# A perceiver layer on one core: written-out engine orders behind the cross-attention, a third score bank, and low parts of two shared blocks on GpSimd

## What is computed

```python
def _L0_xattn_ref(image_features, text_features, Wq, bq, Wk, bk, Wv, bv):
    ...
    scores = jnp.einsum('bqh,bkh->bqk', query, key) * scale
    weights = jax.nn.softmax(scores, axis=-1)
    attended = jnp.einsum('bqk,bkh->bqh', weights, value)
...
def _L0_attn_ref(x, W_dq, W_uq, q_ln_g, q_ln_b, W_dkv, W_ukv, kv_ln_g, kv_ln_b, W_o):
    ...
    cq = _layernorm(x @ W_dq, q_ln_g, q_ln_b)
    Q = cq @ W_uq
    ckv = _layernorm(x @ W_dkv, kv_ln_g, kv_ln_b)
    KV = ckv @ W_ukv
    ...
    scores = scores * mask
    scores = jnp.where(scores == 0, -jnp.inf, scores)
    attn = jax.nn.softmax(scores, axis=-1)
    out = jnp.einsum('bhqk,bkhd->bqhd', attn, v).reshape(B, S, D)
    return out @ W_o.T
...
    x = x + _L0_xattn_ref(_layernorm(x, axis=-1), ctx_768, ...)
    x = x + _L0_attn_ref(_layernorm(x, axis=-1), ...)
    x = x + _L0_ffn_ref(_layernorm(x, axis=-1), ...)
```

## Time and profile before

| | us |
|---|---|
| median of three runs | 369.08 |
| lowest, highest | 368.37, 370.68 |
| the profiled execution | 367.66 |
| its span | 365.9 |
| TensorE busy | 338.9 |

### The profile page before, as it was taken

One profiled execution on the slowest core, in us unless ns is written; L12 is line 12 of the kernel. 1 busy time (PEld: TensorE's weight loads), 2 busy tenths in 40 slices (PEclk: granted clock), 3 DMA queues, 4 the chain that ended last, 5 costly groups with the idle time before them and its releaser, 6 DMA issues.

```text
span 365.9 us, 6976 instructions
## 1 busy us (share of the span) xinstructions
PE 338.9 (93%) x2530; PEld 237.4 (65%) x2530; DVE 244.2 (67%) x481; ACT 190.9 (52%) x429; POOL 83.2 (23%) x103
## 2 busy tenths in 40 slices
PE   5999989999999989987959789999999999999996
PEld 3998666677777767766748667988644444444344
DVE  1874879646588467647675665993436677778587
ACT  2466675526557476355555561522036677777520
POOL 3600000000010211402332304004337544432000
PEclk9999999999999999998978899999999999999999
DMA  7984499976322246055000056479935553331573
GB/s 233 375 322 166 153 391 419 387 231 233 111 88 87 89 134 269 29 219 241 3 28 0 31 172 261 198 275 420 377 141 180 169 174 126 117 107 59 199 291 115
DMA packets 17185, 69.70 MB, mean 190 GB/s; under 512 B 2816, under 2 KB 3328, under 8 KB 14592
## 3 DMA queue, kind: packets, MB, share of 16 engines
q1 hardware_dynamic: 12768, 56.93, 41.7%
q0 software_dynamic: 3520, 11.54, 8.9%
q10 hardware_dynamic: 864, 0.79, 0.7%
HBM read 61.91 MB, written 7.34 MB: 189 GB/s over the span
## 4 chain that ended last, share of the span: by engine, by line
PE 76%; DVE 11%; ACT 6%; issue 3%; DMA 2%; POOL 1%; ACTq 0%; DVEq 0%
PE bank L1802 10%; PE bank L1388 10%; PE bank L1770 10%; PE bank L1390 9%; PE bank L1389 9%; PE bank L1643 8%; PE bank L1739 2%; ACT hw L831 2%; PE bank L1531 2%; PE bank L1781 2%; PE bank L1813 2%; DVE cT L1147 2%; DMA bq_s<-in_bq 2%; PE bank L1613 2%; PE bank L1541 1%
## 5 line engine op out<-in xcount | busy, mean ns | idle before, releaser
L1643 PE MATMUL bank<-ring,wT 128*128 128x384 f32 x128 | 44.0, 487 | 1.2 <-ACT wT L787 1.2
L1802 PE MATMUL bank<-WX,hsT 128*32 128x512 f32 (+1 forms) x128 | 38.2, 598 | 0.0
L1770 PE MATMUL bank<-WX,xsT 128*32 128x256 f32 (+1 forms) x256 | 37.9, 380 | 0.0
L1147 DVE TENSOR_TENSOR cT<-ring_T,cT 128x512 fp32r<-128x512 f32 x48 | 30.5, 686 | 6.4 <-ACT cT L694 6.4
L1643 PEld LDWEIGHTS bank<-ring,wT 128*128 128x128 f32 x128 | 23.6, 190 | 14.7 <-ACT wT L787 1.4
L582 POOL TENSOR_TENSOR rstd<-var,mhalf 128x1 f32<-128x1 f32 x12 | 7.6, 637 | 105.7 <-DVE var L945 105.7
L1770 PEld LDWEIGHTS bank<-WX,xsT 128*32 128x32 f32 x256 | 17.9, 110 | 21.0 <-issue 10.7
L1320 DVE COPY down_copy<-WX 128x1024 f32 x32 | 21.0, 697 | 15.2 <-PE bank L1802 15.2
L1802 PE MATMUL bank<-down_copy,hsT 128*32 128x512 f32 x192 | 30.7, 598 | 0.0
L1770 PE MATMUL bank<-up_copy,xsT 128*32 128x256 f32 x384 | 30.5, 379 | 0.0
L694 ACT CAST cT<-ring_T 128x512 fp32r<-128x512 f32 x48 | 26.8, 618 | 4.8 <-PE bank L1390 4.8
(11 more groups left out here) (287 smaller groups left out, 870.2 us busy)
## 6 DMA issues: line engine op xcount, KB each, us to landing
WX<-in_experts SPq DMA_DIRECT2D x16, 1024.0 KB, 7.1
ring_T<-in_ctxT SPq DMA_DIRECT2D x16, 768.0 KB, 6.9
ring<-in_ctx SPq DMA_DIRECT2D x16, 768.0 KB, 4.8
WX<-y_rows SPq DMA_DIRECT2D x4, 1024.0 KB, 8.7
raw<-in_experts SPq DMA_DIRECT2D x3, 1024.0 KB, 5.3
raw<-in_wqT SPq DMA_DIRECT2D x4, 256.0 KB, 6.2
res<-in_x SPq DMA_DIRECT2D x4, 256.0 KB, 7.4
raw<-in_woT SPq DMA_DIRECT2D x1, 1024.0 KB, 5.4
```

What stands on the lines that cost most here:

```text
L1147: V_.tensor_tensor(cT[:, g % 2, 1, t, :], ring_T[:, g % RING_T, t, :], f32(cT[:, g % 2, 0, t, :]), ALU.subtract).then_inc(cTlo_ok, 1)
L1643: last = mm(bank[B_O][:, 0:TD], wT[:, g % 2, k * P:(k + 1) * P], ring[:, g % RING, k, :], start=(c == 0 and k == 0), stop=(c == NCH - 1 an ...
L1770: last = mm(bank[B_H[g % 2]][q * SLOT:(q + 1) * SLOT, 0:IC * P], xsT[:, g % 2, c * P + q * SLOT:c * P + (q + 1) * SLOT], w, start=c == 0, ...
L1802: last = mm(bank[B_Y[g % 2]][q * SLOT:(q + 1) * SLOT, :], hsT[:, g % 2, m * P + q * SLOT:m * P + (q + 1) * SLOT], w, start=m == 0, stop=m ...
```

## The change

The loop ends at `TAIL` = G + LAG = 21 on all engines. Behind it each of TensorE, VectorE, ScalarE and GpSimd gets a list of calls, one after the other, of the same pieces of work (the loop's code has become functions). Scores of units from 8 on rotate over three banks (4, 0, 6) instead of two, so a pair waits for the exponentials up to unit u - 2 (`exp_ok` at u - 1). Projection 2 goes to bank 1 instead of 2. The low parts of blocks 0 and 1 are written by GpSimd in halves of 512 columns with semaphores of their own. VectorE keeps block 2's; SyncE's loads of blocks 2 and 3 and TensorE's waits follow the new semaphores. Places of `u_w` 0 and 1 are swapped. The diff without the moved functions:

```diff
-        u_w = [at(f"u_w{e}", [P, 2, HALF], wx_place((12, 6, 3, 13)[e]), F32R) for e in range(NSH)]
+        u_w = [at(f"u_w{e}", [P, 2, HALF], wx_place((6, 12, 3, 13)[e]), F32R) for e in range(NSH)]
...
-            return 1 if b < NB // 2 else B_S
+            return 1 if b < NB - 1 else B_S
+
+        def wo_bank(b):
+
+            return 1 if b == NB - 2 else B_S
...
-        UP_SPLIT, DOWN_SPLIT = (25, 26), (28, 30)
-        UP_STEP = ((26, 27), (28, 28))
-        DOWN_STEP = ((30, 31), (31, 32))
-
+        TAIL = G + LAG
...
-            return 0 if u % 2 else 6
+            return (6, B_O, 0)[u % 3 - 2] if u >= 2 * ROWS else 0 if u % 2 else 6
...
-                sp.wait_ge(u_lo, e + 1)
-                sp.wait_ge(d_lo, e + 1)
+                sp.wait_ge(ulo_first, 2 * e + 2)
+                sp.wait_ge(dlo_first, 2 * e + 2)
...
+            def half_low(part, e, h, hi_ok, lo_ok):
+                pool.wait_ge(hi_ok, e + 1)
+                o = (h + 2 * (part is d_part)) * HALF // 2
+                c = slice(h * HALF // 2, (h + 1) * HALF // 2)
+                nc.gpsimd.tensor_tensor(part(e, 1)[:, c], raw[:, e % 2, o:o + HALF // 2], f32(part(e, 0)[:, c]),
+                                        ALU.subtract).then_inc(lo_ok, 1)
...
+            unit_weights(7)
+            inverse_root(norm_no["middle", 3])
+            unit_weights(8)
+            half_low(u_part, 0, 0, u_hi, ulo_first)
+            inverse_root_2(3)
+            unit_weights(9)
+            half_low(u_part, 0, 1, u_hi, ulo_first)
+            unit_weights(10)
+            last_rows(1)
+            half_low(d_part, 0, 0, d_hi, dlo_first)
+            unit_weights(11)
+            half_low(d_part, 0, 1, d_hi, dlo_first)
+            for u in range(12, 16):
+                unit_weights(u)
+            last_rows(2)
+            for h in range(2):
+                half_low(u_part, 1, h, u_hi, ulo_first)
+            for h in range(2):
+                half_low(d_part, 1, h, d_hi, dlo_first)
+            last_rows(3)
...
-                for e in range(FIRST):
-                    if step == UP_STEP[e][1] + 1:
-                        squares_half(e, 0)
-                    if step == UP_SPLIT[e]:
-                        up_hi(e)
-                    if step == DOWN_SPLIT[e]:
-                        down_hi(e)
...
+            sums_hi(3)
+            unit_copy(6)
+            unit_copy(7)
+            unit_exp(8)
+            attended_hi(1)
+            rows_hi(norm_no["middle", 3], 3, bank[B_POST])
+            unit_exp(9)
+            up_hi(0)
+            act_e.wait_ge(att_mm, NB)
+            down_hi(0)
+            compressed(3)
+            unit_exp(10)
+            head_features(3)
+            unit_copy(8)
+            unit_exp(11)
+            values_copy(3)
+            unit_copy(9)
+            unit_exp(12)
+            unit_copy(10)
+            router_exp(0)
+            rows_hi(norm_no["last", 1], 1, bank[rows_bank(1)])
+            unit_copy(11)
+            unit_exp(13)
+            attended_hi(2)
+            unit_copy(12)
+            unit_exp(14)
+            router_exp(1)
+            squares_half(0, 0)
+            unit_copy(13)
+            unit_exp(15)
+            up_hi(1)
+            unit_copy(14)
+            rows_hi(norm_no["last", 2], 2, bank[rows_bank(2)])
+            unit_copy(15)
+            act_e.wait_ge(wo_mm, 2)
+            down_hi(1)
+            attended_hi(3)
+            squares_half(1, 0)
+            router_exp(2)
+            for e in range(FIRST, NSH):
+                up_hi(e)
+                if e < NSH - 1:
+                    down_hi(e)
+            rows_hi(norm_no["last", 3], 3, bank[rows_bank(3)])
+            router_exp(3)
...
-                for e in range(FIRST):
-                    if step == UP_STEP[e][1] + 2:
-                        gated_half(e, 0)
-                    if step == UP_SPLIT[e]:
-                        up_lo(e)
-                    if step == DOWN_SPLIT[e]:
-                        down_lo(e)
...
+            l1, l2, l3 = (norm_no["last", b] for b in range(1, NB))
+            m3 = norm_no["middle", 3]
+            sums_lo(3)
+            inverse_sums(7)
+            mask_and_max(8)
+            cross_added(3)
+            find_masked(9)
+            inverse_sums(8)
+            normalise(m3, 3)
+            put_lowest(9)
+            highest(9)
+            rows_lo(m3, 3, bank[B_POST])
+            attended_lo(1)
+            find_masked(10)
+            moments_2(3)
+            put_lowest(10)
+            normalise_2(3)
+            highest(10)
+            inverse_sums(9)
+            self_added(1)
+            mask_and_max(11)
+            moments(l1, 1)
+            inverse_sums(10)
+            normalise(l1, 1)
+            mask_and_max(12)
+            inverse_sums(11)
+            rows_lo(l1, 1, bank[rows_bank(1)])
+            mask_and_max(13)
+            inverse_sums(12)
+            mask_and_max(14)
+            attended_lo(2)
+            inverse_sums(13)
+            mask_and_max(15)
+            inverse_sums(14)
+            gated_half(0, 0)
+            inverse_sums(15)
+            self_added(2)
+            moments(l2, 2)
+            normalise(l2, 2)
+            rows_lo(l2, 2, bank[rows_bank(2)])
+            attended_lo(3)
+            gated_half(1, 0)
+            self_added(3)
+            moments(l3, 3)
+            normalise(l3, 3)
+            up_lo(FIRST)
+            rows_lo(l3, 3, bank[rows_bank(3)])
+            down_lo(FIRST)
+            dve.wait_ge(d_lo, 1)
...
-                pe.wait_ge(u_lo, e + 1)
+                pe.wait_ge(ulo_first, 2 * e + 2)
...
+            def first_down(e, b):
+                pe.wait_ge(dlo_first, 2 * e + 2)
+                pe.wait_ge(g_ok, e + 1)
+                if e == 0:
+                    pe.wait_ge(rexp_ok, NB - 1)
+                    pe.wait_ge(exp_ok, UNITS)
+                down_tile(e, b, first=e == 0)
...
-                if u >= 2:
+                if u > 2 * ROWS:
+                    pe.wait_ge(exp_ok, u - 1)
+                elif u >= 2:
                     pe.wait_ge(exp_ok, u)
...
+            sums_T(3)
+            pair_scores(8)
+            attended(3)
+            unit_T(6)
+            unit_T(7)
+            unit_sums(1)
+            rows_T(norm_no["middle", 3], bank[B_POST])
+            pair_scores(10)
+            compress(3)
+            project(1)
+            compressed_T(3)
+            unit_T(8)
+            keys_and_queries(3, TAIL)
+            pair_scores(12)
+            unit_T(9)
+            values(3)
+            unit_T(10)
+            router(0)
+            unit_T(11)
+            pe.wait_ge(rexp_ok, 1)
+            rows_T(norm_no["last", 1], bank[rows_bank(1)])
+            pair_scores(14)
+            unit_sums(2)
+            unit_T(12)
+            router(1)
+            first_up(0, 0)
+            unit_T(13)
+            first_up(0, 1)
+            project(2)
+            unit_T(14)
+            unit_T(15)
+            rows_T(norm_no["last", 2], bank[rows_bank(2)])
+            unit_sums(3)
+            for m in range(IC):
+                first_up(1, m)
+            router(2)
+            project(3)
+            first_down(0, 1)
+            first_down(0, 0)
+            rows_T(norm_no["last", 3], bank[rows_bank(3)])
+            first_down(1, 1)
+            router(3)
+            first_down(1, 0)
```

395 lines of the change are left out of this document (212 added, 183 removed).

## The result

The changed kernel took 372.43 us (median of 11 runs, 371.92 to 374.3), the kernel before, beside it, 369.35 us (11 runs, 368.01 to 370.81): ratio 1.0095, 95% interval 1.0073 to 1.0118. The forecast was 368.1 us with 363.6 to 371.5: the time lies outside and on the other side. It is where rival 2 put it (372.2 us, chance 0.14).

What follows compares the result with a forecast made beforehand. TensorE's idle time and low clock between about 159 and 225 us bound the kernel. Walk's gain 3.6 - 2.6 for low clock = 1.0 us: profiled 367.66 to 366.7, plus 1.4 for the median, 368.1 us; range 363.6 to 371.5.

Steps and rivals of the forecast that it cites:

- rival 2: Low clock takes all three dense places (first up quarters, block 1, compression), kernel slower: 372.2 us, chance 0.14.
- The walk at the high clock: Written orders walked from 159.5 us at high clock throughout: second halves and routing start 3.6 us early.
- The first place: Dense blocks behind TensorE's idle 189.5 to 192.1 us: low clock for 3.4 us, charged at half chance, 0.9 us.
- The second place: Dense blocks behind TensorE's mostly idle 200.7 to 207.4 us: low clock for 3.4 us, charged in full, 1.7 us.
- Rival 1: Clock stays high behind TensorE's waits: gain 3.6 to 5.0 us, 365.5 to 364.1 us, chance 0.35.
- the hand-on through the squares: ScalarE's squares_half(0, 0), ahead of exponential 15, passes 3.3 us lost before projection 2 on to the last unit.
- Rival 3: VectorE, in order, is what scores wait for despite the third bank: 369.1 to 370.1 us, chance 0.16.
- The port: VectorE and GpSimd SBUF instructions exclude each other: block 3's low part delays down_lo(2), routing starts 222.7 instead of 221.1 us.
- Edits counted at nothing: Low parts moved from VectorE to GpSimd (4.8 us), swapped u_w, SyncE's earlier release of expert block 2: no gain.
- The expected signs: Trace marks if right, among them scores 12 near 179, projection 3 near 212 to 214, first r_one near 223 to 225 us.

Runs made afterwards that it cites:

- e5: Changed kernel with 74 idle matmuls, results unread, in TensorE's waits, useful order untouched: 368.49 us, ratio 0.9945 to the kernel before.
- e2: Changed kernel with mask_and_max(13) and inverse_sums(12) on VectorE ahead of rows_lo(last, 1): ratio 1.0082 to the kernel before.
- e10: Changed kernel with mask 13 ahead of rows_lo(last, 1), first squares behind exponential 15, block 2's low parts moved, no idle matmuls: 370.93 us, ratio 1.0002 to the kernel before.
- e6: Kernel before with idle matmuls in TensorE's waits, its order untouched: ratio 1.0009 to the kernel before.
- e1: Changed kernel with squares_half(0, 0) behind unit_exp(15) and gated_half(0, 0) behind batch 2's moments: ratio 1.0136 to the kernel before.
- e8: Changed kernel with two score banks instead of three: ratio 1.0368 to the kernel before.
- e3: Changed kernel with VectorE's two low parts of block 2 moved earlier, away from GpSimd's low part of block 3: ratio 1.0147 to the kernel before.
- e11: e5 with the low parts of blocks 0 and 1 on VectorE as whole blocks, not GpSimd halves: ratio 0.9938 to the kernel before.
- e14: e10 with idle matmuls and the low parts of blocks 0 and 1 on VectorE as whole blocks: 364.43 us, ratio 0.9872 to the kernel before.
- e12: Kernel before with the third score bank alone, its order untouched: ratio 0.9930 to the kernel before.

## Why the prediction was wrong

**The walk at the high clock was right, to 1.4 us.** e5 is the walked order with the clock held behind the compression. Walked and measured: projection 2 at 197.3 and 197.72 us, transposes 15 at 202.6 and 203.14, rows 2 at 204.4 and 204.84, projection 3 at 211.65 and 212.55, second halves at 222.3 and 223.69. Of the last 1.4 us, 0.63 us is a wait for GpSimd's low part in front of block 1. Mask 13 was walked to 188.6 and came at 189.13 in e5 (189.71 in the changed kernel), the wait ahead of it as described. A half low part took 1.27 us, taken at 1.19.

**The step that failed** is "I charge the second in full (1.7 us), the first at half chance (0.9 us). 3.6 - 2.6 = 1.0 us." The mechanism was there, the size of its first term wasn't. The first place, charged with 0.9 us, cost 4.3 us: 0.6 in front of transposes 12 and 3.7 from there to projection 2 (e5 against the changed kernel). The low clock held for 13.6 us in one stretch there (187.5 to 201.2 us), not for 3.4. The second place was low for 6.8 us, not 3.4, and yet cost 1.3 us, about the 1.7 charged. Together 5.6 us against 2.6. Why the first stretch is so long stays open: with the same order up to there it was 6.8 us in e2 and 13.6 us in e10.

**The place was wrong too.** The charge stood behind the wait for weights 12 (189.5 to 192.1 us), but the clock had fallen at 187.5 us, so that this wait shrank to 0.84 us. What lay before were waits of 1.85 and 0.98 us (in front of transposes 10 and 11) with transposes and the router's 16-column matmuls between them. The prediction says that before each fall TensorE mostly waited. That isn't so for the longest one of the kernel before, at 188.3 us. TensorE's timeline there:

```profile
186.28 0.66 PE L1541 MATMUL bank<-ident,hw 128*128 128x128 f32 x4
...
187.92 0.26 PE L1390 MATMUL bank<-gate_h,xT_l 128*128 128x16 f32 x1
190.74 1.12 PE L1541 MATMUL bank<-ident,hw 128*128 128x128 f32 x4 [2.56 <-POOL hw L608]
```

From scores 12 (185.19 us) to 188.18 us it was busy without a gap, with scores, transposes and the router; the wait of 1.88 us stood before that, the one of 2.56 us came with the clock already low. The walk looked for falls behind long waits only. (Its count of three stages with a clock below 1 in the earlier trace rows leaves out a fourth, 0.99, the end of that fall.)

**And the gain was counted against the wrong mark.** The walk's 3.6 us compare an order at the high clock with an old trace that pays for 13.6 us at the low one. I said that its times "already hold that", and left it there; e6 shows the old order gains 1.7 us from fillers too. Ledger at the second halves: new order against old with fillers 0.6 us early (223.69, 224.25); clock 5.6 us for the new, 1.7 us for the old; 5.6 - 1.7 - 0.6 = 3.3 us late. It must give the 3.4 us of the profiles, since it is made of them; what it divides is checked only by the medians, 3.1 us apart.

**Rival 1** (the clock stays high) was the more likely one at 0.35 and didn't happen. **Rival 2** did, with its kind and its blocks, though the clock fell 2 us before the place that it named and the hand-on through the squares was worth at most 1.0 us (e1). That its sum meets the time to 0.2 us (372.2 us against 372.43) is partly luck: it charged 3.3 us at the first place, where 4.3 were measured, 1.7 at block 1, where it was 1.3, and 1.7 at the compression, which no run prices by itself. Its chance of 0.14 is the second error: the prediction itself held against rival 1 that two of the walk's idle stretches are as long as those before the falls. **Rival 3** is refuted by e8.

**The port** was right in mechanism and in size: walked, it makes the routing 1.6 us late (222.7 for 221.1 us); measured, `down_lo(2)` takes 3.42 instead of 1.22 us and the routing starts at 229.85 us, 1.7 us behind the router's exponential, which ends at 228.17. `down_lo(2)` started 0.06 us behind GpSimd's low part and ended 1.1 us behind it. In the earlier trace rows the blocked one was GpSimd, which had started second; here it is VectorE, second by 0.06 us. The Trainium skill, SBUF — State Buffer, "Who interferes with whom", says that issue order decides who is blocked; the trace agrees both times. At the end it cost 0.27 us (e3), since TensorE was as late as the routing.

**Edits counted at nothing** were that, within the noise: low parts on GpSimd (e11, e14). The expected signs hold too: scores 12 near 179 us with mask 12 at 182.10, VectorE idle 184 to 189 us, ScalarE waiting for TensorE before the first `act`. Those that failed, projection 3 at 218.13 us and the first `r_one` at 229.85, stand behind the clock.

## What to carry to other kernels

Where a trace shows the granted clock falling, walk an order twice, with the clock high and with the dense blocks at half speed, and take into the second walk blocks behind short waits and narrow matmuls too (the fall at 187.5 us had waits of 1.85 and 0.98 us before it); compare with the old order walked in the same two ways. Before judging a reordering, put idle matmuls into the waits of both versions: it tells what the order is worth (here about 0.6 us) from what the clock does to it (5.6 and 1.7 us), and may be kept (e14, 1.3% faster). Look for falls behind the stretch as well: one at the entries took back 1.5 us of e6's gain. Try each part of a bundle alone: the third bank by itself was the gain (e12, 0.7%), and the order around it gave that back.
